# Score tiles of an attention in two sets of PSUM banks instead of one, in a token-pruning block with experts

## The reference

```python
x_merge = jnp.concatenate([src_unm, dst_merged], axis=1)      # Mn = 1097 tokens per image
q, k, v = ...                                                 # 8 heads of 8 channels each
attn = jnp.einsum('bhqd,bhkd->bhqk', q, k) * SCALE
kth = jax.lax.top_k(attn, Mn // 8)[0][..., -1:]               # the 137th largest of each row
attn = jnp.where(attn >= kth, attn, -jnp.inf)
attn = jax.nn.softmax(attn, axis=-1)
x_attn = jnp.einsum('bhqk,bhkd->bhqd', attn, v)
```

## Time and profile before

| | us |
|---|---|
| three runs | 12219.48, 12256.19 (median), 12288.64 |
| profiled execution, device time | 12231.48 |
| its span | 12229.6 |

### The profile page before, as it was taken

The page is one execution under the profiler, slowest core; times in us unless marked ns, Lnnn a source line. Parts: engine busy times, 40 slices in busy tenths (PEclk is TensorE's granted clock), DMA queues, the critical chain, the costliest instruction groups (busy, mean ns, idle before and its releaser), DMA issues. The chain is left out here.

```text
span 12229.6 us, 166452 instructions
## 1 busy us (share of the span) xinstructions
PE 8209.9 (67%) x45521; PEld 5308.0 (43%) x45521; DVE 9274.5 (76%) x26006; ACT 6990.4 (57%) x11527; POOL 2163.8 (18%) x1960
## 2 busy tenths in 40 slices
PE   4555577776575764767777677776576757344799
PEld 4555455554243432434444344443343434243587
DVE  8999544443898888989989889998889989655243
ACT  0000022112797975979999799997797979322222
POOL 2333211111000000000000000000000000077676
PEclk9999955555566655656666666665566666555555
DMA  3222100000000000000000000000000000143221
GB/s 90 71 76 63 31 22 19 20 19 21 11 17 12 18 11 12 16 12 17 17 15 18 14 14 18 18 14 14 15 14 14 18 12 15 29 96 85 54 58 40
DMA packets 669888, 351.94 MB, mean 29 GB/s; under 512 B 587281, under 2 KB 605680, under 8 KB 665056
## 3 DMA queue, kind: packets, MB, share of 16 engines
q1 hardware_dynamic: 607920, 242.84, 9.2%
q0 software_dynamic: 58624, 60.72, 1.9%
q10 hardware_dynamic: 2384, 37.11, 0.9%
HBM read 200.20 MB, written 147.72 MB: 28 GB/s over the span
## 5 line engine op out<-in xcount | busy, mean ns | idle before, releaser
L1040 PE MATMUL a_psT<-a_qt,a_kt 74*122 74x366 bf16 x3456 | 1556.8, 450 | 800.0 <-ACT a_pT L1120 558.5
L1270 DVE TENSOR_SCALAR_CACHE_REDUCE a_s<-a_psS 122x512 f32<-122x512 f32 (+1 forms) x2304 | 1605.3, 728 | 445.9 <-PE a_psS L1023 310.2
L1128 ACT ACTIVATE a_junk<-a_s,a_aim 122x1097 bf16<-122x1097 f32 x1152 | 1384.9, 1210 | 825.5 <-DVE a_s L1270 822.7
L1120 ACT ACTIVATE a_pT<-a_psT 122x732 f32<-122x732 f32 (+1 forms) x1920 | 1372.1, 715 | 598.3 <-PE a_psT L1043 594.4
L1204 DVE MAX8 a_near<-a_below 122x8 f32<-122x274 f32 (+1 forms) x4608 | 1699.3, 430 | 0.1
L1043 PEld LDWEIGHTS a_psT<-a_weigh,a_drops 122*122 122x122 bf16 x10368 | 1573.4, 191 | 193.0
L1197 DVE SCALAR_TENSOR_TENSOR a_below<-a_s,a_te,a_signs 122x1097 f32<-122x1097 f32 x1152 | 1546.4, 1352 | 128.7 <-remote 127.9
L1043 PE MATMUL a_psT<-a_weigh,a_drops 122*122 122x122 bf16 x10368 | 1527.9, 274 | 0.0
L1056 PE MATMUL a_psO<-a_pT,a_v 122*32 122x366 f32 x6912 | 1415.3, 704 | 0.0
L1128 ACT ACTIVATE a_signs<-a_s,a_te 122x1097 bf16<-122x1097 f32 x1152 | 1401.4, 1219 | 4.4 <-DVE a_te L1189 4.4
L1128 ACT ACTIVATE a_junk<-a_s,a_te 122x1097 bf16<-122x1097 f32 x1152 | 1385.1, 1205 | 0.0
(11 more groups left out here) (348 smaller groups left out, 14305.7 us busy)
## 6 DMA issues: line engine op xcount, KB each, us to landing
xbuf<-r_blank ACTq DMA_DIRECT2D x16, 1990.6 KB
e_xg<-xbuf SPq DMA_DIRECT2D x56, 568.8 KB
r_bc<-pr SPq DMA_DIRECT2D x16, 1372.0 KB, 7.4
a_k<-kT SPq DMA_DIRECT2D x384, 51.5 KB
a_q<-qT SPq DMA_DIRECT2D x384, 51.5 KB
a_kt<-kT SPq DMA_DIRECT2D x384, 51.5 KB
a_qt<-qT SPq DMA_DIRECT2D x384, 51.5 KB
r_xt<-in_x SPq DMA_DIRECT2D x16, 784.0 KB
```

The lines of the kernel that those rows point to most:

```text
L1040: pe.matmul(out[:, x, 0:CW], kt[q][:, u * QP:(u + 1) * QP], qt[q][:, c * CW:(c + 1) * CW], start=True, stop=False)
L1120: act.activation(pT[j % RING][:, 0:w, :], psT[(q + j) % 2][:, 0:w, 0:CW], ACT.Exp).then_inc(exped, 1)
L1128: act.activation(out[:, :], s_[:, t, :], ACT.Sign, bias=at[:, t:t + 1], scale=-1.0, accum_out=total[:, t:t + 1]).then_inc(counted[r], 1)
L1270: dve.tensor_scalar(sc[o][:, t, a:b], psS[0:QP, a:b], 1.0, None, ALU.mult, ALU.max, accum_out=peaks[:, i, t:t + 1]).then_inc(evacuated, 1)
```

## The change

A helper `score_banks` returns the PSUM space of a score tile's two halves: for even tiles the columns of `psS` as before, for odd tiles the two buffers of `psT`, each seen as 1024 columns (lower half in the first, upper half in the second). `score` writes there and `evacuate` reads there.

The waits follow. A half of tile t now waits for the evacuation of the same half of tile t-2, except tile 0, which waits as before for the last tile of the step before. Tile 1 waits also for all exponentials of head s-2, since these read `psT`. In turn the first fills of a step, which write `psT`, wait until tile 7, the last odd one, is evacuated.

```diff
+        def score_banks(t):
+            if t % 2:
+                return (psT[i][:, :, :].rearrange("p x n -> p (x n)") for i in range(2))
+            return psS[0:QP, 0:HALF], psS[0:QP, HALF:3 * HALF]
...
-                wait(pe, evacuated, 2 * n - 1)
+                if t == 1 and last:
+                    wait(pe, exped, SLOTS * (s - 1))
+                wait(pe, evacuated, 2 * n - 1 if t == 0 else 2 * n - 3)
...
-                pe.matmul(psS[0:QP, 0:HALF], q_, ks[o][:, 0:HALF], start=True, stop=True).then_inc(scored, 1)
+                low, high = score_banks(t)
+                pe.matmul(low[:, 0:HALF], q_, ks[o][:, 0:HALF], start=True, stop=True).then_inc(scored, 1)
...
-                wait(pe, evacuated, 2 * n)
+                wait(pe, evacuated, 2 * n if t == 0 else 2 * n - 2)
...
-                pe.matmul(psS[0:QP, HALF:2 * HALF], q_, ks[o][:, HALF:2 * HALF], start=True, stop=True)
-                pe.matmul(psS[0:QP, 2 * HALF:MN], q_, ks[o][:, 2 * HALF:MN], start=True, stop=True).then_inc(scored, 1)
+                pe.matmul(high[:, 0:HALF], q_, ks[o][:, HALF:2 * HALF], start=True, stop=True)
+                pe.matmul(high[:, HALF:MN - HALF], q_, ks[o][:, 2 * HALF:MN], start=True, stop=True).then_inc(scored, 1)
...
                 if last:
+                    wait(pe, evacuated, 2 * QT * done(s + 1) - 2)
                     for i in range(2):
                         fill(s - 2, p, i)
...
+                banks = tuple(score_banks(t))
                 for i, (a, b) in enumerate(((0, HALF), (HALF, MN))):
                     wait(dve, scored, 2 * (QT * (s + 1) + t) + i + 1)
-                    dve.tensor_scalar(sc[o][:, t, a:b], psS[0:QP, a:b], 1.0, None, ALU.mult, ALU.max,
+                    dve.tensor_scalar(sc[o][:, t, a:b], banks[i][:, 0:b - a], 1.0, None, ALU.mult, ALU.max,
```

## The result

The changed kernel took 11953.6 us (median of 4 runs, 11943.4 to 11961.1) beside 12248.8 us for the kernel before (4 runs, 12219.5 to 12288.6). The profiled execution took 11958.8 us, 272.6 us less than the one before; the other 22 us lie between executions that were not profiled.

The account below looks back on a forecast made before the run. VectorE's work plus its waits for TensorE was taken to bound the step. 12231.5 - 195 + 5 = 12041 us from the profiled execution, 12066 from the median; forecast 12060, own range 12020 to 12110, wider range 11985 to 12180.

Parts of the forecast that it names:

- What bounds the kernel: In the attention, a step lasts as long as VectorE's own work and its waits for TensorE, not ScalarE.
- How many: Score stage: 63% of line 1270's 310.2 us of waits for line 1023 goes, 195 us, bounds 0 and 310.2.
- The size of one wait: Score tiles 1 to 7, low clock: 1.68 us per tile, two passes of 0.69, the remaining 0.29 a wait.
- Tile 0: Upper half of a step's first score tile: its wait stays, change 0, bounds 0.4 us a step either way.
- The larger-gain rival: Around tile 0's wait TensorE's clock is granted high more often: 51 us more, 12010 us; chance 0.06.
- The added waits: Tile 1 waiting for all exponentials and the first fills waiting for tile 7: cost 0 each.
- What is late next: After the change VectorE's step is 50.24 us, ScalarE's 49.68, under it by 0.56, so VectorE still ends the step.
- The 5 us given back for ScalarE: Allowance of 5 us in all for attention steps in which ScalarE, not VectorE, ends the step.
- ScalarE's takeover: Rival: all 2.7 us of ScalarE's fill waits per step stay, only 77 us are won, 12179 us; chance 0.13.
- no gain: Rival: all 2.03 us a step come back as longer wait of tile 0's upper half, 12256 us; chance 0.05.
- slower: Rival: TensorE loses its high clock in the fills of exponentials 6 to 14, 154 us more, 12410; chance 0.03.

Follow-up runs that it names:

- the first experiment: The changed kernel with only the lower halves of odd tiles in psT, all upper halves in psS: 12261.5 us against 12257.6 for the kernel before, ratio 0.9998.

## Why the prediction fell short

*What bounds the kernel: right.* VectorE's work and its waits for TensorE made up the step, and the change, which took such waits away, shortened the step by as much as the score stage (2.24 and 2.25 us). The closed loop of the upper half was the cause, as the first experiment shows by bringing it back.

*How many: right by its own measure.* The waits of line 1270 for line 1023 were to fall from 310 to about 115 us. They fell from 310.2 to 111.1. Idle time fell by 209 us where 195 had been put.

*The size of one wait: wrong, and this is the step that failed.* The prediction said "The two passes need 0.69 us each. The rest, 0.29 us, is a wait". It took the upper pass by the time to the next pass, 0.69 us, though its row is 0.77 long, and the lower pass by its row, 0.69, which holds the accumulator row. The lower pass hands over after 0.61 us when the next half is ready. So a tile waited 0.38 us at the low clock (1.68 - 1.30), and 0.09 at the high one, where the prediction said "the wait is gone"; a tile now takes 1.30 us and not "1.39 us at either clock". The waits of the upper halves of tiles 1 to 7, put at 195 us, were worth 292 us by the starts of the passes. The missing part is the accumulator rows: seven tiles of 128 steps with 0.083 us each are 74 us, most of the 83 us by which VectorE's busy time fell, and idle and busy time together fell by 209 + 83 = 292 us. The rest of the 83 us are rows that got shorter (6.7 us in sum) and small differences. 16 us were lost in the later stages of the profiled execution, which the change doesn't touch. The range was built around the idle column, and no rival had a gain outside it.

*Tile 0: right within its bounds.* Its wait stayed, 111.1 us in all against 37% of 310.2, or 115, before. From its lower to its upper half it takes 0.08 us a step longer in the mean, where 0 had been put. The larger-gain rival, which had put its hope there, was the wrong way to a larger gain.

*The added waits: right.* The wait for all exponentials and the one for tile 7 cost VectorE and ScalarE nothing. The first fill of the step above:

```profile
6162.08 0.53 PE L1049 MATMUL a_psT<-a_qt,a_kt 74*122 74x366 bf16 x1 [0.78 <-DVE a_s L1281]
```

It waited 0.78 us for tile 7, whose accumulator row is at 6161.66, and came 0.42 us after it. Before, tile 8's upper matmul stood between the two. ScalarE's wait ahead of the first exponential fell all the same, from 0.71 to 0.40 us a step.

*What is late next: right in the order, with the wrong place.* ScalarE was near, and it first showed at the threshold move ahead of tile 8, 0.2 us in the changed kernel and up to 0.9 us once tile 0's waits had been moved about. "VectorE still waits for nothing of ScalarE" missed that. The 5 us given back for ScalarE were needed, and too few: some 11 us went there. ScalarE's takeover, no gain and slower are all refuted by the ratio of 0.976. The clock stayed at 0.61 and ScalarE's fill waits fell, so the slower rival's condition never arose. The Trainium skill (TensorE: Matmul & The Clock Gate, "HAM oscillation — how this bites in real kernels") reports of one matmul kernel that double-buffering PSUM gave no further gain. Taken as a rule for this kernel it does not hold: here the second set of banks gave 2.4%.

## What to carry to other kernels

Take the cost of a wait from the period with it and the period without it, not from the idle column: find one instance of the same pair in the trace that had nothing to wait for, here tile 8, and subtract. When two engines share one buffer, add up the loop (pass, release, refill, handover) for each part of it; doubling one part uncovers the loop of the next, and doubling both opens them. When a wait goes and the time stays, look first at what now stands ahead in the same queue, before you name another engine.

## What the runs showed of the hardware

A VectorE pass with an accumulator output is two rows. The following pass starts at the start of the accumulator row, 0.61 us after a 512-column pass began, if its data is ready. If it has to wait it starts later, and there is no fixed step in between: before the change there are starts after 0.66, 0.70 and 0.98 us, and in the run in which only tiles 1 and 3 use psT there is one after 0.63. The first 0.08 us of such a wait are shown as busy, since the accumulator row fills them. The 0.61 us held in tiles 1 to 7 of all 128 steps of the changed kernel, for passes over psS and over psT, and in the run in which all nine tiles are read from psS.
